# A macaron layer with experts on one core: every product in plain fp32, and a dispatch that goes tile by tile

## The reference

```
x = x + 0.5 * ffn(layernorm(x))
x = x + attention(layernorm(x))
x = x + 0.5 * ffn(layernorm(x))        # the same weights as the first

ffn(x):   shared = (silu(x Wg0^T) * (x Wu0^T)) Wd0^T             # inner width 256
          probs  = sigmoid(x R^T + routing_bias)                 # 8 experts
          the best 2 experts of each row, weights scaled to sum 1
          out    = shared + sum over the row's two experts e of
                   weight * ((silu(x Wg_e) * (x Wu_e)) Wd_e)     # inner width 256
attention(x): q, k, v = x Wq^T + bq, x Wk^T, x Wv^T + bv ; 16 heads of 8
          phi(a) = silu(a * 8**-0.25) + 1 for q and k
          kv  = phi(k)^T v for each head and each sequence of 256 rows
          out = (phi(q) kv) Wo^T + bo
```

## Time and profile before

| | |
|---|---|
| median of 3 runs | 795.73 us (795.63 to 799.72) |
| profiled execution, own time | 798.22 us |
| its span (first to last instruction) | 796.5 us |
| mean granted TensorE clock | 0.921 of full |
| busy: PE, PEld | 682.1 us, 639.2 us |
| busy: DVE, ACT, POOL | 571.3 us, 471.7 us, 533.0 us |
| DMA | 89.40 MB, 112 GB/s over the span |

### The profile page before, as it was taken

The page is one execution under the profiler, slowest core; times in us unless marked ns, Lnnn a source line. Parts: engine busy times, 40 slices in busy tenths (PEclk is TensorE's granted clock), DMA queues, the critical chain, the costliest instruction groups (busy, mean ns, idle before and its releaser), DMA issues. The chain is left out here.

```text
span 796.5 us, 17786 instructions
## 1 busy us (share of the span) xinstructions
PE 682.1 (86%) x5133; PEld 639.2 (80%) x5133; DVE 571.3 (72%) x1886; ACT 471.7 (59%) x866; POOL 533.0 (67%) x564
## 2 busy tenths in 40 slices
PE   7574979772799999999789889999778999999990
PEld 6464869662799999999678788888677999999990
DVE  7778787771355787877688988899875555777672
ACT  5353453331467777786657666866425677777760
POOL 1457777777777777776166666777774577777672
PEclk9778788987899999999799999999979999999995
DMA  9312221141544555552122111111333535666545
GB/s 278 123 52 77 81 64 55 55 145 54 156 132 125 157 170 166 156 156 58 51 62 67 41 38 45 45 44 51 86 105 83 146 104 149 208 207 200 184 144 168
DMA packets 63337, 89.40 MB, mean 112 GB/s; under 512 B 13194, under 2 KB 43788, under 8 KB 63244
## 3 DMA queue, kind: packets, MB, share of 16 engines
q1 hardware_dynamic: 46348, 53.37, 23.4%
q0 software_dynamic: 16896, 34.90, 13.1%
HBM read 46.10 MB, written 42.12 MB: 111 GB/s over the span
## 5 line engine op out<-in xcount | busy, mean ns | idle before, releaser
L608 POOL DMA_INDIRECT x_rows<-send,send_to x256 | 248.5, 971 | 135.9 <-issue 71.6
L620 POOL DMA_INDIRECT y_rows<-send,y_to x272 | 264.2, 971 | 100.7 <-issue 73.7
L1637 DVE TENSOR_TENSOR h<-silu_g,u_bank 128x512 f32<-128x512 f32 x136 | 93.5, 687 | 114.3 <-ACT silu_g L758 107.8
L733 ACT ACTIVATE slot_gu<-w_gu 128x1024 fp32r x130 | 137.8, 1060 | 36.8 <-issue 36.7
L1013 PE MATMUL y_bank<-w_dn,h 128*128 x1088 | 143.7, 275 | 0.1
L1013 PEld LDWEIGHTS y_bank<-w_dn,h 128*128 128x128 f32 x1088 | 133.2, 192 | 0.3 <-issue 0.3
L855 PE MATMUL g_bank<-xT_hi,slot_gu 128*128 128x256 f32 x260 | 85.8, 330 | 9.9 <-DVE xT_lo L1628 9.2
L928 PEld LDWEIGHTS y_bank<-w_dn,h 128*128 128x128 f32 x512 | 69.2, 212 | 23.3 <-issue 20.6
L928 PE MATMUL y_bank<-w_dn,h 128*128 128x128 f32 x512 | 70.1, 296 | 19.0 <-DVE x L1234 19.0
L758 ACT ACTIVATE silu_g<-g_bank 128x512 f32<-128x512 f32 x136 | 78.8, 579 | 12.0 <-PE g_bank L857 11.5
L677 ACT ACTIVATE send<-x,shift,rstd 128x128 f32<-128x128 f32 x128 | 52.6, 482 | 37.7 <-DVE shift L1196 26.1
(11 more groups left out here) (270 smaller groups left out, 1626.0 us busy)
## 6 DMA issues: line engine op xcount, KB each, us to landing
send<-x_rows SPq DMA_DIRECT2D x130, 130.0 KB
y_pair<-y_rows SPq DMA_DIRECT2D x32, 512.0 KB
y_rows<-send,y_to POOLq DMA_INDIRECT x272
x<-x_in SPq DMA_DIRECT2D x16, 256.0 KB, 7.3
x_rows<-send,send_to POOLq DMA_INDIRECT x256
out<-x SPq DMA_DIRECT2D x16, 256.0 KB
w_raw<-w_experts SPq DMA_DIRECT2D x15, 256.0 KB, 3.1
x_rows<-pad SPq DMA_DIRECT2D x16, 130.0 KB, 2.4
```

The costliest lines, as they stand in the source:

```text
L608: pool.indirect_dma_start(x_rows, bass.IndirectOffsetOnAxis(ap=send_to[b % SEND_TO_RING][:, w, k:k + 1], axis=0), send[ring_of(f, t)][:, w ...
L620: pool.indirect_dma_start(y_rows, bass.IndirectOffsetOnAxis(ap=y_to[k][:, j:j + 1], axis=0), y_out[f][k][:, j, :], None).then_inc(y_sent[k ...
L733: act.activation(slot_gu[n % 2][:].rearrange("p a n -> p (a n)"), w_gu[:, bass.ds(e, 1)].rearrange("p e a n -> p (e a n)").bitcast(F32), A ...
L1637: dve.tensor_tensor(h[par][0][:], silu_g[par][:], u_bank[par][:], ALU.mult).then_inc(slot_h_done, 1)
```

## The change

All products are plain fp32 now: `three`, `high`, `low` and all splits are gone. ACT copies the transposed rows once (`copy_xT`, `copy_slot_xT`) and a slot's weights at half the width (`copy_slot_weights`, also for mixed slots, which had their weights loaded by SP from DRAM). Experts 1 to 8 come in one early load into `w_gu`, where eight loads went through `w_raw`. The router has one matmul of 8 columns for each 128 rows. Routing has 25 steps, as the two halves of the logits need no addition. The table `BATCHES` now has 16 batches of one tile for the first dispatch too.

```diff
-BATCHES = (((0,), (1,)) + tuple((t, t + 1) for t in range(2, TILES, 2)),
-           tuple((t,) for t in range(TILES)))
+BATCHES = (tuple((t,) for t in range(TILES)),) * 2
-ROUTE_STEPS = 26
+ROUTE_STEPS = 25
...
-            sp.wait_ge(pad_ready, 1)
+            sp.dma_start(w_gu[:, 1:, :], w_experts[1:, :, 0:2 * INNER].rearrange("e p n -> p e n")).then_inc(experts_loaded, 16)
...
-            for e in range(1, EXPERTS):
-                wait_count(sp, split_lo, 0 if e == 1 else split_expert(e - 2))
-                sp.dma_start(w_raw[e % 2][:], w_experts[e, :, 0:2 * INNER]).then_inc(w_loaded[e % 2], 16)
...
-            def three(bank_ap, w_parts, x_parts):
-
-                pe.matmul(bank_ap, w_parts[0], x_parts[0], start=True, stop=False)
-                pe.matmul(bank_ap, w_parts[0], x_parts[1], start=False, stop=False)
-                return pe.matmul(bank_ap, w_parts[1], x_parts[0], start=False, stop=True)
...
-                    pe.matmul(logits, xT_hi[t % XT_RING][:, s], router_parts[:], start=True, stop=False)
-                    last = pe.matmul(logits, xT_lo[t % XT_RING][:, s], router_parts[:], start=False, stop=True)
+                    last = pe.matmul(route_bank[:, (i + j) * ROUTED:(i + j + 1) * ROUTED], xT[t % XT_RING][:, s], router_w[:],
+                                     start=True, stop=True)
...
-                three(g_bank[k][:], (w[:, 0, g], w[:, 1, g]), xs)
-                three(u_bank[k][:], (w[:, 0, u], w[:, 1, u]), xs).then_inc(gu_psum, 1)
+                pe.matmul(g_bank[k][:], w[:, g], xT[par][:], start=True, stop=True)
+                pe.matmul(u_bank[k][:], w[:, u], xT[par][:], start=True, stop=True).then_inc(gu_psum, 1)
...
-                pe.wait_ge(slot_lo_done, full_before(n + 1))
-                pe.wait_ge(slot_gu_done, full_before(n + 1))
+                pe.wait_ge(slot_xT_done, n + 1)
+                pe.wait_ge(slot_w_done, n + 1)
...
-                        last = three(bank_[:, c * ROWS:(c + 1) * ROWS], (w[:, 0, i], w[:, 1, i]), xs)
+                        for j, w in enumerate(weights):
+                            k = c * ROWS + j * width
+                            last = pe.matmul(bank_[:, k:k + width],
+                                             w[par][:, base + c * P:base + (c + 1) * P],
+                                             xT[par][:, j * width:(j + 1) * width], start=True, stop=True)
...
-            def low(item):
-                hi, lo = xT_of(item)
-                dve.wait_ge(xT_hi_done, TR[item] + 1)
-                dve.tensor_tensor(lo[:], tr_bank[:], hi[:].bitcast(F32), ALU.subtract).then_inc(xT_lo_done, 1)
```

More of the change, by code:

```diff
@@ L80 @@
 FIRST_STEPS, TABLE_STEPS = 19, 60
-TABLE_PIECES = {"last tile": (1, 8), "dispatched": (8, 22), "low": (22, 29), 0: (29, 35), 1: (35, 41)}
+TABLE_PIECES = {"last tile": (1, 8), "dispatched": (8, 22), "first slot": (22, 29), 0: (29, 35), 1: (35, 41)}
 TWO_BANKS_FROM = 2 * TILES - 2
@@ L381, in mixed @@
             return n % slots in MIXED_AT
-        def mixed_before(n):
-            return sum(mixed(m) for m in range(n))
-        def full_before(n):
-            return n - mixed_before(n)
         def entry(s):
@@ L635, in _, with copy_xT @@
         def _(act):
[L636 to L640 removed]
+            def copy_xT(item):
                 kind, f, t = item
@@ L972, in slot_gate_up @@
                 par = n % 2
-                pe.wait_ge(slot_lo_done, full_before(n + 1))
-                pe.wait_ge(slot_gu_done, full_before(n + 1))
+                weights = slot_w if mixed(n) else slot_w[0:1]
+                width = ROWS // len(weights)
+                pe.wait_ge(slot_xT_done, n + 1)
+                pe.wait_ge(slot_w_done, n + 1)
                 wait_count(pe, slot_h_done, n - 1)
@@ L1287, in route @@
-                    if step == 7:
+                        op = dve.tensor_tensor(pick[:, step // 11, 0:n], grid(best), wide(first_best), ALU.is_equal)
+                    if step == 6:
                         op = dve.scalar_tensor_tensor(out=grid(rest), in0=pick[:, 0, 0:n], scalar=OUT_OF_RANGE, in1=grid(z),
                                                       op0=ALU.mult, op1=ALU.add)
+                    if step == 12:
+                        op = dve.tensor_tensor(mask[len(ts)][:, 0:n, :], pick[:, 0, 0:n], pick[:, 1, 0:n], ALU.add)
@@ L1298, in route @@
                     if step == 17:
-                        op = dve.reciprocal(picks(score_recip), picks(score_safe))
-                    if step == 18:
                         dve.wait_ge(ranks_psum, batch_no(f, b) + 1)
@@ L1656, in slot_stage @@
                         slot_results(f, s - 2)
-                    if s + 1 < slots:
-                        slot_low(f, s + 1)
                     if s == 0:
-                        table_piece(f, "low")
-                    if f == 0 and s == slots - 1:
-                        low((ATTN, 1, 0))
+                        table_piece(f, "first slot")
                     slot_multiply(f, s)
@@ L1751, in middle @@
                         mask_heads(i)
-                    if 0 <= i < tiles - 2:
-                        low((ATTN, 1, i + 2))
                     if 0 < i + 1 < tiles:
```

262 lines of the change are left out of this document (76 added, 186 removed).

## The result

| | before | changed |
|---|---|---|
| median of the runs side by side, us | 797.30 (4 runs) | 819.85 (4 runs) |
| profiled execution: own time, span, us | 798.2, 796.5 | 819.2, 817.5 |
| slot 6 of the first half starts, us | 202.7 | 207.8 |
| slots 13 to 67, first half, us | 138.8 | 153.3 |
| middle: slot 67 to slot 8 of the second half, us | 257.6 | 241.0 |

The changed kernel is slower: ratio 1.0281, 95% interval 1.0246 to 1.0316. The forecast was 823 (806 to 838), with 0.87 for slower. The total is right within 4 us; the difference between the kernels, +27.4 by the forecast's sum, is +21.0 by the spans. It came out near by way of two misses of opposite sign, which are the subject of most of what follows.

The account below looks back on a forecast made before the run. Bounds: POOL in the first dispatch, PE in both slot stages (POOL almost as full), DVE in the middle's late-pick turns. Terms -4.5 +1.5 +17 +20.3 -2 -4.9 sum to +27.4 us; from the 795.73 median, 823, range 806 to 838.

Parts of the forecast that it names:

- first dispatch (start of slot 6): First dispatch: single tiles let POOL run without a hole from the second tile, ending earlier; -4.5 us.
- first slots, 6 to 13: First slots after the dispatch: weight loads go, longer slots and a slow clock at the start cost; +1.5 us.
- slots, first half: First slot stage: 55 full slots at 2.87 us where they had 2.51, less 2.3 of stalls; +17 us.
- middle: Middle turns: DVE's 13.26 us becomes 11.85, PE becomes the bound at 12.6; sum -2 us, ends -8 and +11.
- slots, second half: Second slot stage: 58 full slots, each 0.35 us longer on PE; +20.3 us.
- tail: End of the kernel: POOL no longer lags and needs 2.8 us after the last results; -4.9 us.
- load-bound rival: Fp32 records bound by weight load, below 0.18 us at 256 columns, so slots keep their length; 774 us, chance 0.10.
- 8.6 us. That is below POOL's 10.18: First dispatch: DVE's cost per single tile, with a quarter of the four-tile norm, is under POOL's time per tile.
- so POOL runs on from 39.3: First dispatch: POOL issues DMAs without a gap from the second tile, ending at 192.4 against 198.1; -5.7, taken as -4.5.
- the dispatch starves: First dispatch: PE's longer products at half clock delay tiles' ranks, ending 4 to 8 us later; 833 us, chance 0.10.
- six or seven turns of 13.3: Middle: DVE-bound turns with late picks, expected to fall to 12.6 us each; -4.7 us.
- the 12.6 that I took as PE's floor: Middle: PE's work in a turn grows from 11.8 to 12.6 us and sets the turn's length.

Follow-up runs that it names:

- kernel 1: Changed kernel with the first dispatch by pairs of tiles again; 814.29 us, ratio 1.0185 to the kernel before.
- kernel 6: Changed kernel with DVE's norm of four tiles done one or two tiles earlier in the first dispatch; 815.55 us, ratio 1.0221 to the kernel before.
- Kernel 2: Kernel before with each three-matmul product made one plain fp32 product of high parts, all subtractions kept; 836.91 us, ratio 1.0474.
- kernel 3: Kernel before without DVE's subtractions for the low parts of x, the high part standing in for them in three F32R products; 780.85 us, ratio 0.9772.
- kernel 7: Kernel 4 without the slots' low-part subtraction, the high part of x used instead; 788.04 us, ratio 0.9884 to the kernel before.
- kernel 4: Kernel before with plain products and no low parts in dispatch (by pairs) and middle, three F32R products in the slots; 793.11 us, ratio 0.9929.
- kernel 5: Kernel before with the first dispatch tile by tile, products still in three F32R parts; 808.0 us, ratio 1.0119.
- kernel 8: Kernel before with plain fp32 products and no low parts of x in the middle alone; 793.17 us, ratio 0.9944.

## Why the prediction was right, and where it was not

| term | forecast | measured | off by |
|---|---|---|---|
| first dispatch (start of slot 6) | -4.5 | +5.2 | +9.7 |
| first slots, 6 to 13 | +1.5 | +2.2 | +0.7 |
| slots, first half | +17 | +14.6 | -2.4 |
| middle | -2 | -16.6 | -14.6 |
| slots, second half | +20.3 | +17.8 | -2.5 |
| tail | -4.9 | -2.2 | +2.7 |
| sum | +27.4 | +21.0 | -6.4 |

**Full slots: right.** Columns decide the price of an fp32 record, and the mixed slot was the right row to read it from. The load-bound rival is dead: 0.216 us where it needed less than 0.18. The term was some 2.4 us too large in each half. Of that 1.7 is 0.03 us too much on a slot (2.87 for 2.84). The rest is a matter of where I cut: the term counted 55 and 58 full slots, but between the transposes of the table PE does gate and up of 53 and 56, and the other two fall into the rows of the middle and of the tail.

**First dispatch: wrong in sign.** The step that failed is "8.6 us. That is below POOL's 10.18", and with it "so POOL runs on from 39.3". I spread the norm of four tiles evenly over four tiles and compared sums of busy time. But a tile's ranks come at the end of a chain through DVE, ACT, PE and DVE, and with single tiles POOL holds at most one tile of work in front of it, so every lump in that chain comes out as a gap. A pair gives POOL 20 us of work at a time, and covers the lumps: before and kernel 1 run through from the third tile. My rival "the dispatch starves" had the place and the sign (it gave +4 to +8, measured +5.2), but only half the reason, half clock on PE. Kernels 1 and 6 put 3.5 us on the single tiles and 2.8 on the place of the norm, which overlap. Kernel 2 puts 4.7 on the longer products: they delay the third tile's start from 55.25 to 58.93. Single tiles cost 10.5 with the old products and 3.5 with the new, so the removed splitting does pay. In pairs it depends on the products: with the old ones the low parts of x gave nothing back (kernel 3: +0.3), with the plain ones kernel 1, which has none of the splitting, is 3.0 ahead of kernel 2, which has all of it.

**Middle: the turns half right, the way out missed.** Late turns came out as worked out, 12.64 us (six of eight) and bound by PE, +4.5 in all (forecast +3.2). The early ones gave 10.3 us where I had 5.5. I had misread them: "six or seven turns of 13.3" and one of 15 were in fact 10.6, 13.5, 12.1, 16.0, 12.4, 13.3 and 16.8. The two longest shrank by some 3 each, and three of the seven are now below the 12.6 that I took as PE's floor (9.1, 12.0 and 11.4). The larger part was not in the sum at all. It ended with the fifteenth turn, and the 56 us from there to slot 8 I held as fixed, without a term; they lost 11.9, although seven full slots in them are 0.33 us longer each. (The way in, from slot 67 to the first turn, took 1.1 more.) The rows show 4.6 us of PE waiting for one subtraction, which stood behind the tables in DVE's queue, and some 3 of half clock behind it; 2.6 of waits for the last tile's low part; and 3 for loads of rows, 0.2 after. The granted clock of the passage is 0.88 before and 1.00 after.

How the 11.9 divide between the two halves of the edit is not to be read from this passage alone: kernel 3 has -4.8 and kernel 2 -3.8 there, and what is missing can't be the slots' low part, which kernel 3 lacks as well. The eight late turns and the way out are better taken together: 150.0 us before, 142.6 changed, 151.2 in kernel 2 and 142.4 in kernel 3. Without the low parts they are 7.6 shorter, with plain products alone 1.2 longer, and with both 7.4 shorter, which adds up within 1. Plain products lengthen the late turns by 4.5 to 5.0 and get most of it back behind them; kernel 3 comes out of its shorter turns (91.4) sooner and then waits 4.3 us for loads of rows, where the changed kernel waits 0.2. What sets those loads was not tried.

**Tail: mis-sized.** I forecast no lag of POOL and 2.8 us behind the last result. POOL has indeed caught up at 794.59, where it waits for a result. But the last three results come at 796.22, 798.39 and 799.57, not 2.84 apart, while POOL needs 2.54 for each; their six DMAs run without a hole from 797.40 to 804.74. That is 4.75 us behind the end of the last result, against 7.75 before: the lag that I had at 2.8 was mis-sized by 2, and the table's row also holds two longer slots.

**Chances.** 0.87 for slower rested on the slots, and these did decide: +32.4 us. For the rest -9.9 was forecast and -11.4 came, but only because the dispatch and the middle, 10 and 15 us off, nearly cancelled.

## What to carry to other kernels

A change that speeds one engine at another's cost is to be costed in every stage, the short passages between two loops too: the largest gain here, 11.9 us, was in a passage that no term covered (4.5 of it makes up for late turns that had become longer). Ask of each removed instruction what stands ahead of it in its queue and who waits behind it; its own length (0.42 us against a wait of 4.64 and half clock after it) says little, and the wait isn't won in full either, as the next one stands behind it (3.0 us in kernel 7). An average of busy time per item below the limit does not keep an engine fed: look for the largest lump between two items, and for how much work is queued in front of the engine when it comes. And a choice of precision can differ by stage: plain products where VectorE is the bound and three F32R ones where TensorE is gave 0.993 of the time before, by kernel 4 (0.9905 to 0.9953): a small gain.

## What was not expected of the hardware

- From 128 columns up the fp32 product goes by its columns and the clock: a record of 128 columns takes 0.112 us, eight of 256 columns 1.73 us at full clock (236.64 to 238.37), and a product of 512 columns, two records, 0.85 us at full clock (523.61 to 524.46) and 1.71 at the low one (100.90 to 102.61). Below that it doesn't: the router's four products of 8 columns, eight records, take from 521.85 to 522.66, 0.10 us for each. So a record has a least price, as the load-bound rival had it, but it lies near that of 128 columns.
- Kernels 4, 5, 7 and 8 have full slots of 2.52 to 2.55 us or small stalls where before has 2.51 to 2.53, with the same instructions. The F32R records start 0.118 us apart in kernels 4 and 7 and 0.119 in kernel 8, instead of 0.117. Their buffers lie elsewhere in memory; whether that is the cause wasn't tried. Differences of 1 to 2 us in a stage of 150 are therefore not to be read as effects of an edit, and this holds for the 1.9 us of kernel 8's dispatch too.
